# RK4 stage: VectorE seeds the couplings in PSUM in place of TensorE's identity matmuls, and w and the scaled copies of P move in their queues

## What is computed

```
def _derivative(q, p, drive, coupling, bias):
    i_couple = jnp.tanh(q) @ coupling.T
    dq = q - q ** 3 / 3.0 - p + drive + i_couple + bias
    dp = EPSILON * (q + ALPHA - BETA * p)
    return (dq, dp)

def _rk4_step(q, p, drive, coupling, bias):
    dq1, dp1 = _derivative(q, p, drive, coupling, bias)
    dq2, dp2 = _derivative(q + 0.5 * DT * dq1, p + 0.5 * DT * dp1, drive, coupling, bias)
    dq3, dp3 = _derivative(q + 0.5 * DT * dq2, p + 0.5 * DT * dp2, drive, coupling, bias)
    dq4, dp4 = _derivative(q + DT * dq3, p + DT * dp3, drive, coupling, bias)
    q_next = q + DT / 6.0 * (dq1 + 2 * dq2 + 2 * dq3 + dq4)
    p_next = p + DT / 6.0 * (dp1 + 2 * dp2 + 2 * dp3 + dp4)
    return (jnp.clip(q_next, -CLAMP, CLAMP), jnp.clip(p_next, -CLAMP, CLAMP))
...
(_, _), q_trace_tbn = jax.lax.scan(scan_fn, (q0, p0), drive_tbn)
```

## Time and profile before

| | us |
|---|---|
| median of 3 runs | 895.88 |
| lowest and highest | 895.19, 896.51 |
| the profiled execution | 899.47 |
| its span, first to last instruction | 897.7 |
| one RK4 step in it | 5.87 |

### The profile page before, as it was taken

How to read it: one execution, slowest core, us unless ns; L and a number is a source line. 1 busy time by engine, 2 the same in 40 slices (tenths; PEclk the granted TensorE clock), 3 DMA queues, 4 the chain that set the end, 5 groups by cost and what they waited for, 6 DMA issues and landing times.

```text
span 897.7 us, 18535 instructions
## 1 busy us (share of the span) xinstructions
PE 887.3 (99%) x7192; PEld 766.1 (85%) x7192; DVE 598.7 (67%) x1700; ACT 413.5 (46%) x1147; POOL 299.1 (33%) x386
## 2 busy tenths in 40 slices
PE   9999999999999999999999999999999899999998
PEld 7788788888888888888888878899987699999998
DVE  5555555654565544656476775777787888888887
ACT  3234222342223432224356664555545766666665
POOL 1765510121101301024614415343223555654343
PEclk9999999999999999999999999999999999999999
DMA  7222000000000000110014000000000000000000
GB/s 277 92 67 88 25 1 1 2 1 1 2 1 1 1 1 1 48 48 2 1 31 169 1 0 1 1 2 1 1 1 2 0 2 25 2 24 2 25 1 26
DMA packets 5705, 22.02 MB, mean 25 GB/s; under 512 B 880, under 2 KB 1264, under 8 KB 5232
## 3 DMA queue, kind: packets, MB, share of 16 engines
q1 hardware_dynamic: 5616, 20.82, 6.6%
HBM read 18.72 MB, written 2.10 MB: 23 GB/s over the span
## 4 chain that ended last, share of the span: by engine, by line
PE 92%; DVE 4%; ACT 2%; DMA 1%; issue 1%; SPq 0%; POOL 0%; DVEq 0%; ACTq 0%
PE ps L372 47%; PE ps L780 8%; PE ps L784 7%; PE ps L640 7%; PE ps L461 6%; PE ps L779 5%; PE ps L630 3%; PE ps L642 3%; PE ps L450 2%; DMA ada_sb<-ada_w 1%; DVE Pr L1252 0%; DVE yt L1663 0%; PE ps L646 0%; DVE BD L1259 0%; DVE frs L1273 0%
## 5 line engine op out<-in xcount | busy, mean ns | idle before, releaser
L1218 DVE TENSOR_SCALAR qk<-ps,vec 128x512 f32<-128x512 f32 x64 | 48.1, 751 | 99.1 <-PE ps L372 99.0
L372 PE MATMUL ps<-x_hi,W_hi 128*128 128x512 f32 x256 | 102.7, 401 | 2.2 <-DVE V L1225 1.8
L873 ACT ACTIVATE qk<-ps,vec 128x512 f32<-128x512 f32 x64 | 44.2, 690 | 129.9 <-PE ps L372 129.9
L372 PE MATMUL ps<-x_lo,W_hi 128*128 128x512 f32 x256 | 100.6, 393 | 0.0
L372 PE MATMUL ps<-x_hi,W_lo 128*128 128x512 f32 x256 | 100.5, 393 | 0.0
L780 PE MATMUL ps<-rk_th,cpc 128*128 128x128 f32 x516 | 99.0, 294 | 0.2
L1229 DVE SCALAR_TENSOR_TENSOR o_lo<-ps,vec,o_hi 128x512 fp32r<-128x512 f32 x64 | 47.1, 744 | 69.1 <-ACT o_hi L889 65.8
L889 ACT ACTIVATE o_hi<-ps,vec 128x512 fp32r<-128x512 f32 x64 | 44.0, 687 | 105.8 <-PE ps L461 105.8
L780 PEld LDWEIGHTS ps<-rk_th,cpc 128*128 128x128 f32 x516 | 72.7, 191 | 9.3 <-ACT rk_th L1160 6.1
L779 PE MATMUL ps<-rk_th,cpc 128*128 128x64 f32 x508 | 77.8, 255 | 0.0
L640 PE MATMUL ps<-ht,hh 128*128 128x128 f32 x512 | 77.1, 283 | 0.4 <-DVE ht L1574 0.2
(11 more groups left out here) (293 smaller groups left out, 2144.3 us busy)
## 6 DMA issues: line engine op xcount, KB each, us to landing
stage<-qkv_w SPq DMA_DIRECT2D x6, 768.0 KB, 4.3
stage<-out_w SPq DMA_DIRECT2D x4, 512.0 KB, 3.8
f_raw<-ffn_w SPq DMA_DIRECT2D x2, 1024.0 KB, 4.8
xorig<-xT SPq DMA_DIRECT2D x1, 2048.0 KB, 8.0
x_all<-xT SPq DMA_DIRECT2D x1, 1536.0 KB, 14.5
out<-xtb SPq DMA_DIRECT2D x3, 512.0 KB, 3.1
ada_sb<-ada_w SPq DMA_DIRECT2D x1, 1024.0 KB, 8.7
BD<-qkv_w SPq DMA_DIRECT2D x1, 768.0 KB, 6.6
```

Of the source, the lines that this page charges most:

```text
L372: r = pe.matmul(out_, lhsT, rhs, start=first and i == 0, stop=last and i == n - 1)
L873: act.activation(qk[:, 0, h % 2, :], ps[:, PJ[0], :], ACT.Identity, bias=col("qkv_b", HU * u + h)).then_inc(act_evac, 1)
L1218: dve.tensor_scalar(qk[:, 1, h % 2, :], ps[:, PJ[1], :], col("qkv_b", HEADS + HU * u + h), None, ALU.add).then_inc(dve_evac, 1)
```

## The change

Four edits, all in the RK4 stage.

1. **TensorE.** `linear` is called for evaluation 2 of step 0 alone. Elsewhere the coupling is added straight onto what VectorE has put into the bank. Before each tanh wait, `chunks_in_turn` now issues 2 idle passes, waits for the seed of the next evaluation (`seeded`) and issues 2 more; `chunks_together` issues 5, waits and issues 2.
2. **VectorE, target.** Z2 (from step 1), Z3, Z4 and E1 are written into PSUM, into the banks of their evaluation (`seed(k)`).
3. **VectorE, order.** w1 goes ahead of Z2, w2 ahead of Z3, w4 ahead of P, and E1 between the two halves of `qraw`. s1 now waits for V5 in every step.
4. **ScalarE.** V3 and V5 of step t's P, made so far at the end of step t and the start of step t+1, stand now behind the square of evaluation 1 of step t+1, with V4 behind them. POOL's code is the same but for the count that U3 waits for.

```
-RK_ACT = ("V5", "th1a", "th1b", "sq1", "V4", "th2a", "th2b", "sq2", "th3a", "th3b", "sq3", "Da", "Db", "th4a", "th4b",
-          "sq4", "V3")
+RK_ACT = ("th1a", "th1b", "sq1", "V3", "V5", "V4", "th2a", "th2b", "sq2", "th3a", "th3b", "sq3", "Da", "Db", "th4a", "th4b",
+          "sq4")
...
+            def seeded(t, k):
+                step, name = (t - 1, "E1") if k == 1 else (t, f"Z{k}")
+                pe.wait_ge(rk_dve, RK_START + at(step, RK_DVE, name))
...
                 coupled(k, 1, 1, False, True).then_inc(rk_pe, 1)
+                keep_warm(2)
+                if k == 2:
+                    seeded(t, 3)
+                elif t < T - 1:
+                    seeded(t + 1, 1)
+                keep_warm(2)
...
                 coupled(k, 1, 1, False, True).then_inc(rk_pe, 1)
+                keep_warm(5)
+                seeded(t, k + 1)
+                keep_warm(2)
...
-                    pe.wait_ge(rk_dve, RK_START + at(t - 1, RK_DVE, "E1"))
-                    linear(1, "E1")
                     chunks_together(t, 1)
...
                 if t:
-                    dve_done("P", t - 1)
-                    scaled("V5", K5)
                     tanhs(1, "qraw", t - 1, ("qa", "qb"))
                     dve_done("q")
                     square("q", C_ / 3)
+                    dve_done("P", t - 1)
+                    scaled("V3", K3)
+                    scaled("V5", K5)
                     scaled("V4", K4)
...
-                if t < T - 1:
-                    dve_done("P")
-                    scaled("V3", K3)
...
+            def seed(k):
+                lo = RK_BANK[k % 2][0]
+                return ps[:, lo:lo + KC, 0:B]
...
-                inc(STT(r_["Z4"], r_["q3"], 2 * (1 - A_ * C_), r_["b4"], M, Ad))
+                inc(STT(seed(4), r_["q3"], 2 * (1 - A_ * C_), r_["b4"], M, Ad))
...
                 if t + 1 < T:
-                    act_("V3")
+                    act_("V3", t + 1)
                     TT(r_["U3"], dnext, r_["V3"], ALU.subtract).then_inc(rk_pool, 1)
```

More of the change, by code:

```diff
@@ L88 @@
 RK_START = 3
-RK_ACT_START = 2 - 5
+RK_ACT_START = 2 - 6
 def at(step, events, name):
@@ L778, in coupled @@
                 if last:
-                    return pe.matmul(ps[:, RK_BANK[k % 2][c], 0:B], w, th, start=first, stop=last)
-                return pe.matmul(ps[:, RK_BANK[k % 2][c], 0:2 * B], w, twice(th), start=first, stop=last)
+                    return pe.matmul(ps[:, RK_BANK[k % 2][c], 0:B], w, th, start=first, stop=last, skip_group_check=True)
+                return pe.matmul(ps[:, RK_BANK[k % 2][c], 0:2 * B], w, twice(th), start=first, stop=last, skip_group_check=True)
             def linear(k, z):
                 for c in range(KC):
-                    pe.matmul(ps[:, RK_BANK[k % 2][c], 0:2 * B], ident[:, :], twice(rk[z][:, c, :]), start=True, stop=False)
+                    pe.matmul(ps[:, RK_BANK[k % 2][c], 0:2 * B], ident[:, :], twice(rk[z][:, c, :]), start=True, stop=False, skip_group_check=True)
             def tanh_done(t, k, half):
                 pe.wait_ge(rk_act, RK_ACT_START + at(t, RK_ACT, f"th{k}{half}"))
+            def seeded(t, k):
+                step, name = (t - 1, "E1") if k == 1 else (t, f"Z{k}")
+                pe.wait_ge(rk_dve, RK_START + at(step, RK_DVE, name))
             def chunks_in_turn(t, k):
@@ L1720, in _ @@
                     dve.wait_ge(rk_first, 1 + RK_FIRST.index("sq1"))
+                mine("q")
                 inc(STT(r_["w"], r_["qsq" if t else "w4"], -(C_ + 1), r_["q"], Ad, M))
+                mine("U2")
+                inc(STT(seed(2) if t else r_["Z2"], r_["q"], 1 - A_ * C_, r_["U2"], M, Ad))
                 a1 = coupling(1, 0)
@@ L1730, in _ @@
                     dve.wait_ge(rk_first, 1 + RK_FIRST.index("V5"))
+                else:
+                    act_done("V5")
                 inc(STT(r_["s1"], r_["q"], W1, r_["V5"], M, Ad))
+                act_done("sq2")
+                mine("q2b")
+                inc(STT(r_["w"], r_["qsq"], -C_, r_["q2"], Ad, M))
                 mine("t3")
-                inc(STT(r_["Z3"], r_["q2"], -A_ * C_, r_["t3"], M, Ad))
-                act_done("sq2")
-                inc(STT(r_["w"], r_["qsq"], -C_, r_["q2"], Ad, M))
+                inc(STT(seed(3), r_["q2"], -A_ * C_, r_["t3"], M, Ad))
                 a2 = coupling(2, 0)
@@ L1767, in _ @@
                 inc(STT(half("qraw", 0), a4, 1 / 3, half("w4", 0), M, Su))
+                mine("P")
+                inc(dve.tensor_tensor(seed(1), r_[f"D{(t + 1) % 3}"], r_["P"], Su))
                 inc(STT(half("qraw", 1), coupling(4, 1), 1 / 3, half("w4", 1), M, Su))
@@ L2028, in dve_, with act_ @@
                     pool.wait_ge(rk_dve, RK_START + at(t, RK_DVE, name))
-                def act_(name):
-                    pool.wait_ge(rk_act, RK_ACT_START + at(t, RK_ACT, name))
+                def act_(name, step=t):
+                    pool.wait_ge(rk_act, RK_ACT_START + at(step, RK_ACT, name))
                 if t:
```

25 lines of the change are left out of this document (8 added, 17 removed).

## The result

| | before | after |
|---|---|---|
| median, us | 895.82 | 903.77 |
| lowest and highest | 895.19, 896.51 | 903.61, 903.88 |
| profiled execution, its span | 899.47, 897.7 | 903.61, 901.9 |
| one RK4 step in it | 5.87 | 6.12 |

Four runs of each, ratio 1.009 with an interval of 1.0078 to 1.0102: the change makes the kernel 7.95 us slower. The forecast was 903.0.

A forecast was written before the change was run, and what follows sets the result against it. A loop through four engines, 5.87 us a step, was taken as the bound, not TensorE. POOL's chain 0.21 plus port 0.02 give 0.23 a step, over 31 steps 7.1: 895.9 + 7.1 = 903.0 us, range 896 to 909.

The forecast's parts named there:

- Part 1: TensorE, each step: identity matmuls (2.0 us) go, idle passes (at most 1.5 us) come; gain on the loop 0.
- the thin place: Seed E1 written between qraw's halves: TensorE begins evaluation 1 some 0.1 us behind its tanh, still covered by w1.
- rival 4: Seed waits hold TensorE: evaluation 1 later by 0.1 us, still under w1, same time as the forecast; chance 0.02.
- Part 2: VectorE writes the seeds to PSUM: nothing added, 285 ns into PSUM as into SBUF.
- Part 3: VectorE, w1 ahead of Z2: w1 starts 0.10 us earlier, a gain that vanishes inside the longer step.
- Part 4: V3 behind the square delays POOL's U3, store, U4, m, b4, so VectorE's s2 waits: +0.21 us a step.
- The port: VectorE's t3 and POOL contend for SBUF: U4 may lose 0 to 0.11 us, taken as 0.02 a step.
- Step 0: First RK4 step: its seed comes 0.2 us later, once, half hidden by the warming passes.
- The span: Profiled execution: span after the change near 904.8 us, the earlier profile standing 3.6 above the median.
- rival 3: TensorE loses its clock (0.50) in the RK4 stage: 28 us on top, 931 us; chance 0.03.
- Rival 1: POOL's chain is hidden after all, b4 ending before 750.65: 2.8 us faster, 893.1 us; chance 0.12.
- Rival 2: Gains of 0.07 and 0.10 reach POOL's chain and cancel the loss: 895.9 +- 1.8 us; chance 0.06.

The follow-up runs named there:

- w_first_only: The kernel before with w1 ahead of Z2 and w2 ahead of Z3 on VectorE, nothing else changed: 894.06 us, ratio 0.9984.
- copies_only: The kernel before with only V3, V5 and V4 behind the square of evaluation 1, identity matmuls and VectorE order kept: 903.64 us, ratio 1.009.
- v3_back: The changed kernel with V3 alone back behind the square of evaluation 4: 896.89 us, ratio 1.0015.
- store_first: The changed kernel with POOL's store of q moved ahead of U3: 895.16 us, ratio 0.9998.

## Why the prediction was right, point by point

**The bound (right).** I read a TensorE busy for 99% as not bounding. For the kernel before, w_first_only settles it: the same work on TensorE, all identity matmuls included, fits into a step 0.08 shorter. In the changed kernel TensorE has about 0.5 us of rest a step and nothing is won with it. I called the identity matmuls a quarter of TensorE's time; four groups of 0.50 in 5.87 us are a third, and nothing in the sum hung on it.

**Part 1 (right).** Zero while POOL's chain is the path: with the identity matmuls or without, 6.13 or 6.12 us (copies_only). No run has part 1 alone; from w_first_only to the fastest kernels, with parts 1 and 2 and more, it is 0.03 a step. The idle passes are hidden too: behind them TensorE still waits for tanh, here for the first half of evaluation 4.

```profile
756.67 0.49 PE L780 MATMUL ps<-rk_th,cpc 128*128 128x128 f32 x2 [0.30 <-ACT rk_th L1168]
```

Evaluation 1, the thin place, came as worked out (end of tanh's first half, then start of the coupling):

```profile
757.63 0.26 ACT L1168 ACTIVATE rk_th<-rk_qraw 128x64 f32<-128x64 f32 x1 [0.69 <-DVE rk_qraw L1779]
```

```profile
757.98 0.67 PE L780 MATMUL ps<-rk_th,cpc 128*128 128x128 f32 x4
```

The coupling starts 0.10 behind its tanh in 30 of 31 steps. In the remaining one, the one before the step shown above, E1 itself came 0.24 late and the coupling started 0.34 behind tanh (751.63 to 751.97). Even there `q2` starts 0.40 behind w1, about as `q4` does behind w3, and names no wait for TensorE: the cover held (rival 4 stays without effect).

**Part 2 (right).** The seeds take 0.28 to 0.29 us into two banks of PSUM, as their rows of before did into SBUF.

**Part 3 (right in the main).** w1 starts at qb + 0.83, forecast +0.83 (748.42 less 747.59); `q2` at qb + 1.24, forecast +1.23. The gain vanishes in the changed kernel and shows up wherever POOL's chain is short. Unforeseen was the price at another place: w4 ahead of P makes V3 and with it U3 later, onto q (v3_back). In the changed kernel U3 is behind the square anyway and doesn't meet q.

**Part 4 (right; each link).** Offsets from qb, median over steps:

| | U3 | store | U4 | m | b4 | s2 |
|---|---|---|---|---|---|---|
| forecast | 1.11 | 1.525 | 1.94 | 2.355 | 2.885 | 3.38 |
| after | 1.10 | 1.52 | 1.93 | 2.40 | 2.93 | 3.42 |

The pitch of 0.415 is 0.41, the latency from POOL to VectorE that no row showed is 0.03, not 0.04. One link is off: m comes 0.47 behind U4.

**The port (the term that was mis-sized).** I took 0.02 a step from a range of 0 to 0.11 for what U4 loses to t3. POOL's groups over the steps show it, U4, then U3 and the store, which meet nothing:

```profile
L2053 POOL TENSOR_TENSOR rk_U<-rk_D,rk_V 128x128 f32<-128x128 f32 x29 | 14.7, 506 | 0.0
...
L2063 POOL TENSOR_TENSOR rk_U<-rk_D,rk_V 128x128 f32<-128x128 f32 x29 | 13.2, 456 | 82.7 <-ACT rk_V L1145 82.7
L2036 POOL TENSOR_TENSOR xtb<-xtb,rk_q 128x128 f32<-128x128 f32 x29 | 13.2, 454 | 0.0
```

506 ns against 455: 0.05. And t3 ends 0.24 late (0.53 for 0.29), forecast 0.3. Chain 0.20 and port 0.05 make 0.25 a step where 0.23 was forecast: 31 x 0.25 = 7.7 us, where 7.1 stood. That is 0.6 of the 0.8 us between 903.0 and 903.8.

**Step 0 (right in size, for another reason).** I named 0.2 us of which half is hidden, and left it out of the sum. From U2 to the first qb it takes 6.16 us (702.55 to 708.71) where it took 6.09 (706.06 to 712.15). `q2` comes 0.32 earlier there, since w1 is first, and the rest of the step takes 0.38 longer.

**The span (a miss).** I expected a span near 904.8, because the profiled execution of before stood 3.6 above its median and I carried that over. It is 901.9. The extra was not the change's: nearly all of it lies in the 1.81 us of rest at 94.46 and the half clock behind it, which in 3.30 us loses 1.65. The trace of after has no such rest, nor has its clock a dip:

```profile
95.60:98.90 3.30, 3.30 (x19) 2.83 (x18) 0.75 (x1) 0.69 (x1) 1.05 (x2) 1.00 0.34 124
```

Nineteen matmuls where before had ten. At the end of that stretch the same matmul starts 3.3 us earlier than before, and RK4 begins at 702.55 instead of 706.06, 3.5 earlier. I had quoted that stretch for rival 3 and not seen that it explained the offset. The forecast of the median, a difference added to a median, did not depend on it.

**The rivals.** Rival 1 named a b4 that ends before s2's turn as its point, and a store ahead of U3 as one way to it. store_first shows both, with 895.2 us instead of 893.1; with t3 or V3 placed better as well, 893.7 and 893.6. Rival 2 (both cancel): from the two places that were to go onto POOL's chain nothing came. Rival 3: the clock is at 1.00 in the whole stage of the changed kernel, and in the traced execution without idle passes too. (Its 0.11 for a pass is not four in 0.50; by those it is 0.125, and the rival's price 31 us.)

**What stays open.** Kernels with w1 ahead of Z2 have some single steps that are longer, 0.15 to 0.35 us in about four of 31, in sum 0.9 us against 0.1 to 0.4 with Z2 ahead. In store_first one looks so (w1, Z2, `q2`):

```profile
774.15 0.29 DVE L1730 SCALAR_TENSOR_TENSOR rk_w<-ps,rk_q 128x128 f32<-128x128 f32 x1
774.36 0.28 DVE L1732 SCALAR_TENSOR_TENSOR ps<-rk_q,ps 128x128 f32<-128x128 f32 x1
774.90 0.23 DVE L1735 TENSOR_TENSOR rk_q<-ps,rk_w 128x64 f32<-128x64 f32 x1 [0.25 <-DVE ps L1732]
```

`q2` follows Z2 by 0.54 where 0.19 is usual (768.54 to 768.73), and w1 and TensorE had long been done. In the changed kernel it is hidden behind POOL's chain. What the traces add: over all twelve kernels VectorE is held for 0.24 us or more 40 times in the steps 1 to 30, and 35 of these are followed, 0.65 to 1.05 us after it goes on, by a packet of 8192 bytes in a DMA queue of the kind `instruction`, though there is only one such packet in 14 us. In store_first they end at 749.84, 774.90 and 799.87 us, 25 us apart. Where in a step the hold falls differs between the kernels, and with it whether it reaches the path. That points to the loading of instructions, but no run varied it, so the cause stays open.

## What to carry to other kernels

When a producer is moved back in one engine's queue, write down every operation that stands behind its consumer in the next queue, and follow that list to the first engine that waits for its end: here a copy of 0.29 us made 1.3 us later cost nothing by itself, and four POOL operations behind its reader cost 7.9 us. Then ask which of them could stand ahead: moving one that nobody waits for (the store) took the whole loss back. On a stage whose busiest engine shows 99%, price the edits by the loop of waits and not by that engine's work; and after each reordering look again at which operations of VectorE and POOL now lie over each other.
